# Finish of the attention heads: scaling one head further ahead, output added two heads behind, and a weight ring of eight slots

## The reference, cut to what matters

```python
def xattn(inputs_q, inputs_kv, Wq, Wk, Wv, Wo):
    q = (inputs_q @ Wq).reshape(b, sq, H, HD) * (1.0 / np.sqrt(HD))
    k = (inputs_kv @ Wk).reshape(b, skv, H, HD)
    v = (inputs_kv @ Wv).reshape(b, skv, H, HD)
    attn = softmax(einsum('bqhd,bkhd->bhqk', q, k), axis=-1)
    ctx = einsum('bhqk,bkhd->bqhd', attn, v).reshape(b, sq, H * HD)
    return ctx @ Wo

x = x + xattn(layernorm(x), ctx_2048, Wq, Wk, Wv, Wo)
x = x + linear_attn(layernorm(x), log_decay, ...)   # chunk of 128 rows, gate, group norm
x = x + ffn(layernorm(x), w1, b1, ln_g, ln_b, w2, b2)
```

## Time and profile before

| | before |
|---|---|
| median of 3 runs | 2038.02 us (2037.34 to 2038.19) |
| profiled execution | 2039.78 us |
| its span, first to last instruction | 2037.9 us |
| TensorE busy | 1955.8 us (96%) |
| VectorE busy | 1606.4 us (79%) |
| ScalarE busy | 1127.4 us (55%) |
| GpSimd busy | 272.4 us (13%) |
| mean rate of DMA over the span | 149 GB/s |

### The profile page before, as it was taken

How to read it: one execution, slowest core, us unless ns; L and a number is a source line. 1 busy time by engine, 2 the same in 40 slices (tenths; PEclk the granted TensorE clock), 3 DMA queues, 4 the chain that set the end, 5 groups by cost and what they waited for, 6 DMA issues and landing times.

```text
span 2037.9 us, 46247 instructions
## 1 busy us (share of the span) xinstructions
PE 1955.8 (96%) x17334; PEld 1596.3 (78%) x17334; DVE 1606.4 (79%) x3444; ACT 1127.4 (55%) x2484; POOL 272.4 (13%) x465
## 2 busy tenths in 40 slices
PE   5799999999999999999999999999999999999786
PEld 5577887887887987977978978878878878878462
DVE  4788788788888888888888888888888887877426
ACT  3556566666656555555555565555565556555212
POOL 1011111111111111111111111111111111100001
PEclk8899999999999999999999999999999999999888
DMA  5568887887886888787787887888978877765540
GB/s 147 148 113 163 164 162 153 160 165 153 163 161 133 143 161 162 145 160 156 146 165 156 147 156 156 147 155 162 168 147 157 147 136 142 138 121 128 206 177 6
DMA packets 966945, 304.44 MB, mean 149 GB/s; under 512 B 893985, under 2 KB 952865, under 8 KB 965825
## 3 DMA queue, kind: packets, MB, share of 16 engines
q1 hardware_dynamic: 966720, 301.47, 74.8%
HBM read 72.16 MB, written 4.46 MB: 38 GB/s over the span
## 4 chain that ended last, share of the span: by engine, by line
PE 91%; DVE 5%; DMA 2%; issue 1%; ACT 1%; POOL 0%; DVEq 0%; ACTq 0%; SPq 0%; POOLq 0%
PE ps_v L1211 25%; PE ps_s L1196 24%; PE ps_t L1196 19%; PE ps_w L1211 18%; DMA bulk<-in_vo 1%; PE ps_w L1170 1%; DVE pp L875 1%; PE ps_v L1183 1%; PE ps_t L1290 1%; DVE acc L884 0%; PE ps_s L1333 0%; PE ps_v L1297 0%; DVE prob L870 0%; ACT bulk L602 0%; PE ps_s L1152 0%
## 5 line engine op out<-in xcount | busy, mean ns | idle before, releaser
L1196 PE MATMUL ps_s<-bulk 128*128 128x128 f16 (+2 forms) x4752 | 583.4, 272 | 2.7 <-DVE bulk L811 2.7
L1211 PE MATMUL ps_v<-nring,pt 128*128 128x256 f16 x4704 | 581.4, 273 | 3.0 <-DVE acc L884 1.5
L1211 PEld LDWEIGHTS ps_v<-nring,pt 128*128 128x128 f16 x4704 | 458.8, 98 | 63.7 <-DVE acc L794 2.6
L1196 PEld LDWEIGHTS ps_s<-bulk 128*128 128x128 f16 x4752 | 404.6, 98 | 114.7 <-DVE bulk L811 2.9
L1196 PE MATMUL ps_t<-bulk 128*128 128x384 f16 (+2 forms) x3564 | 454.0, 272 | 18.9 <-ACT ps_t L653 17.2
L1211 PE MATMUL ps_w<-nring,pt 128*128 128x256 f16 x3528 | 451.8, 273 | 8.0 <-DVE ps_w L894 6.4
L875 DVE SCALAR_TENSOR_TENSOR pp<-prob,pp 128x384 f16<-128x384 f32 (+4 forms) x680 | 423.5, 689 | 0.0
L1196 PEld LDWEIGHTS ps_t<-bulk 128*128 128x128 f16 x3564 | 301.8, 98 | 111.6 <-ACT ps_t L653 18.9
L1211 PEld LDWEIGHTS ps_w<-nring,pt 128*128 128x128 f16 x3528 | 340.0, 98 | 57.5 <-DVE ps_w L894 8.6
L633 ACT ACTIVATE pp<-prob 128x384 f16<-128x384 f32 (+4 forms) x680 | 370.9, 623 | 5.5 <-DVE prob L870 4.7
L622 ACT ACTIVATE prob<-ps_s,nmax 128x768 f32<-128x768 f32 (+2 forms) x136 | 119.1, 876 | 431.6 <-DVE nmax L850 424.9
(11 more groups left out here) (187 smaller groups left out, 1410.5 us busy)
## 6 DMA issues: line engine op xcount, KB each, us to landing
stage<-in_ctx SPq DMA_DIRECT2D x196, 128.0 KB, 2.9
wst<-in_w SPq DMA_DIRECT2D x64, 256.0 KB, 3.2
bulk<-in_vo SPq DMA_DIRECT2D x16, 512.0 KB, 6.4
acc<-in_qk SPq DMA_DIRECT2D x11, 512.0 KB, 4.1
pt<-pp SPq DMA_TRANSPOSE x272, 5.6
tern_d<-wter SPq DMA_DIRECT2D x32, 128.0 KB, 2.9
bulk<-tern_d SPq DMA_DIRECT2D x2, 2048.0 KB, 11.1
nring<-in_aw SPq DMA_DIRECT2D x3, 1024.0 KB, 8.4
```

Source lines behind the costliest of these rows:

```text
L1196: ins = mm(out if n == 1 else out.rearrange("p (n m) -> p n m", m=P), q_part(e, qlo, a)[:, c * P:(c + 1) * P], t_moving(k, run, tlo, b, c) ...
L1211: ins = mm(dst, pt[:, tile:tile + P], n_part(c, clo, b), start=(first and n == 0 and plo == 0 and clo == 0), stop=(last and n == w - 1 and ...
```

## The change

It touches only the end of the attention and the loads that feed it.

- VectorE scales heads 0 and 1 before its part of the last step (135), and later head f+2 before it copies head f. `norm_head` waits for the last step of its own pair in place of the last of all.
- TensorE takes `turn(2)` and `finish(1)` ahead of the values of step 134, and `turn(3)` and `finish(2)` ahead of those of step 135. `add_out` runs two heads behind `finish`, and starts at f = 3. `ot` has three buffers, which lie in `part_u`.
- The weight ring has eight slots. The first five are loaded after step 130, three more after step 132, the others when their slot is free. The `aw` matrices but the last are mixed with the next loads; the last, the feed-forward weights and the rows come after all heads' weights. `aw_q` and one of the rows lie in `pt` now.
- The decay matrix's operations come two heads later on VectorE and ScalarE.

```diff
-        un, ut, ot = prob[:, 0:2 * D], prob[:, 2 * D:4 * D], prob[:, 4 * D:4 * D + 2 * P]
-        VO = TRW + 3 * QSW
-        AQ = VO + 4 * SL
+        un, ut, ot = prob[:, 2 * D:4 * D], prob[:, 4 * D:6 * D], part_u[:, 0:3 * P]
+        VO, NVO = TRW + 3 * QSW, 8
         tern = bulk[:, 0:WP * D].bitcast(BF16)
         b1b, lngb = (bulk[:, WP * D + n * F:WP * D + (n + 1) * F] for n in range(2))
-        ring_vo = bulk[:, VO:AQ]
-        lnbb = bulk[:, AQ:AQ + F]
-        aw_q = bulk[:, AQ + F:AQ + F + KC * D]
+        ring_vo = bulk[:, VO:VO + NVO * SL]
+        aw_q, lnbb = (pt[:, n * 2 * F:(n + 1) * 2 * F].bitcast(F32) for n in range(2))
...
+        def last_step(e):
+            return max(k for k, step in enumerate(STEPS) if step[0] == e)
...
             def load_vo(f):
-                if f >= 4:
-                    sp.wait_ge(out_mm, f - 3)
-                sp.dma_start(ring_vo[:, (f % 4) * SL:(f % 4 + 1) * SL], vo_d[Q_ORDER[f]]).then_inc(in_vo[f % 4], 16)
+                if f >= NVO:
+                    sp.wait_ge(out_mm, f - NVO + 1)
+                sp.dma_start(vo_slot(f), vo_d[Q_ORDER[f]]).then_inc(in_vo[f % NVO], 16)
...
-                if k == NS - 2:
-                    sp.wait_ge(s4_done, max(i for i, step in enumerate(STEPS) if step[0] == 5) + 1)
-                    for f in range(4):
+                if k == last_step(5) + 1:
+                    sp.wait_ge(s4_done, last_step(5) + 1)
+                    for f in range(5):
+                        load_vo(f)
+                if k == last_step(7) + 1:
+                    sp.wait_ge(s4_done, last_step(7) + 1)
+                    for f in range(5, NVO):
                         load_vo(f)
...
+            for f in range(NVO, NVO + 3):
+                load_vo(f)
+            sp.wait_ge(v4_done, NS)
             sp.dma_start(aw_q, aw_d[0]).then_inc(in_aw, 16)
-            load_vo(4)
-            sp.wait_ge(v4_done, NS)
-            for n, w in enumerate((aw_k, aw_v, aw_o)):
+            for n, w in enumerate((aw_k, aw_v)):
+                load_vo(NVO + 3 + n)
                 sp.dma_start(w, aw_d[n + 1]).then_inc(in_aw2[n], 16)
-                load_vo(5 + n)
             sp.dma_start(xin, x_d).then_inc(in_xr, 16)
-            load_vo(8)
+            for f in range(NVO + 5, H):
+                load_vo(f)
+            sp.dma_start(aw_o, aw_d[3]).then_inc(in_aw2[2], 16)
             for n in range(2):
                 sp.wait_ge(out_w[n], 16 * WP)
-            for f in range(9, H):
-                load_vo(f)
-                if f in (11, 13):
-                    n = (f - 11) // 2
-                    sp.dma_start(tern[:, n * WP * D:(n + 1) * WP * D].rearrange("p (n d) -> p n d", d=D),
-                                 tern_d[n * WP:(n + 1) * WP].rearrange("n p d -> p n d")).then_inc(in_tern, 16)
+                sp.dma_start(tern[:, n * WP * D:(n + 1) * WP * D].rearrange("p (n d) -> p n d", d=D),
+                             tern_d[n * WP:(n + 1) * WP].rearrange("n p d -> p n d")).then_inc(in_tern, 16)
...
-                if f == 0:
-                    value_a(NS - 2)
-                    value_e_u(NS - 2)
-                    value_a(NS - 1)
-                    value_e_u(NS - 1)
-                if f == 6:
+                if f in (2, 3):
+                    value_a(NS - 4 + f)
+                    value_e_u(NS - 4 + f)
+                if f == 8:
...
-            for k in range(NS):
+            for k in range(NS - 1):
                 step(k)
-            v.wait_ge(lo_done, 5 * NS)
...
-                if f == 0:
-                    v.wait_ge(l_done, 2 * alphas(NS - 1))
+                final = last_step(h // 2)
+                v.wait_ge(l_done, 2 * alphas(final))
                 for g in range(2):
-                    v.wait_ge(acc_done[g], NS - LAG if f < 2 else NS)
+                    v.wait_ge(acc_done[g], final + 1)
...
             def o_copy(f):
                 v.wait_ge(o_mm, f + 1)
-                if f >= 2:
-                    v.wait_ge(out_mm, f - 1)
-                nc.vector.tensor_copy(ot[:, (f % 2) * P:(f % 2 + 1) * P], ps_t[:, (f % 2) * D:(f % 2) * D + P]).then_inc(o_cp, 1)
-
+                if f >= 3:
+                    v.wait_ge(out_mm, f - 2)
+                nc.vector.tensor_copy(ot[:, (f % 3) * P:(f % 3 + 1) * P], ps_t[:, (f % 2) * D:(f % 2) * D + P]).then_inc(o_cp, 1)
+
+            v.wait_ge(lo_done, 5 * (NS - 1))
             norm_head(0)
             norm_head(1)
-            o_copy(0)
-            value_sum_d(NS - 2)
-            value_sum_e(NS - 2)
-            add_values(NS - 2, 1)
-            add_values(NS - 2, 0)
-            value_sum_d(NS - 1)
-            value_sum_e(NS - 1)
-            add_values(NS - 1, 1)
-            add_values(NS - 1, 0)
-            norm_head(2)
-            o_copy(1)
-
-            v.wait_ge(in_const, 16 * 5)
+            step(NS - 1)
...
-            for f in range(2, H):
-                if f + 1 < H:
-                    norm_head(f + 1)
+            for f in range(H):
+                if f + 2 < H:
+                    norm_head(f + 2)
                 o_copy(f)
-                if f < 6:
-                    nc.vector.tensor_tensor(dec3[:, f - 2], diff3, ld3[:, f - 2].to_broadcast([P, 4, P]), ALU.mult).then_inc(dec_p, 1)
-                elif 8 <= f < 12:
+                if f in (1, 2):
+                    k = NS - 3 + f
+                    value_sum_d(k)
+                    value_sum_e(k)
+                    add_values(k, 1)
+                    add_values(k, 0)
+                if 4 <= f < 8:
+                    v.wait_ge(in_const, 16 * 5)
+                    nc.vector.tensor_tensor(dec3[:, f - 4], diff3, ld3[:, f - 4].to_broadcast([P, 4, P]), ALU.mult).then_inc(dec_p, 1)
+                elif 10 <= f < 14:
                     v.wait_ge(dec_e, 1)
-                    nc.vector.tensor_tensor(dec3[:, f - 8], dec3[:, f - 8], mask3, ALU.mult).then_inc(dec_m, 1)
+                    nc.vector.tensor_tensor(dec3[:, f - 10], dec3[:, f - 10], mask3, ALU.mult).then_inc(dec_m, 1)
...
             turn(0)
             turn(1)
             finish(0)
-            values(NS - 2)
-            values(NS - 1)
             for f in range(1, H):
                 if f + 1 < H:
                     turn(f + 1)
                 finish(f)
-                if f == 1:
+                if f in (1, 2):
+                    values(NS - 3 + f)
+                if f == 3:
                     pe.wait_ge(acc_done[1], NS)
-                add_out(f - 1)
+                    pe.wait_ge(acc_done[0], NS)
+                    add_out(0)
+                if f == 4:
+                    add_out(1)
+                if f >= 4:
+                    add_out(f - 2)
+            add_out(H - 2)
             add_out(H - 1)
```

More of the change, by code:

```diff
@@ L252, in alphas, with vo_slot @@
             return sum(visit(i) > 0 for i in range(k + 1))
+        def vo_slot(f):
+            return ring_vo[:, (f % NVO) * SL:(f % NVO + 1) * SL]
+        def last_step(e):
+            return max(k for k, step in enumerate(STEPS) if step[0] == e)
         Q_ORDER = [h for k in range(NP) for h in heads_of(k)]
@@ L259, in perceiver_layer @@
         in_qk = [sem(f"in_qk{k}") for k in range(3)]
-        in_vo = [sem(f"in_vo{k}") for k in range(4)]
+        in_vo = [sem(f"in_vo{k}") for k in range(NVO)]
         in_ctx = sem("in_ctx")
@@ L1281, in finish @@
             def finish(f):
[L1282 to L1283 removed]
+                w = vo_slot(f)
+                pe.wait_ge(in_vo[f % NVO], 16 * (f // NVO + 1))
                 pe.wait_ge(exp_done[1], NS)
```

6 lines of the change are left out of this document (2 added, 4 removed).

## The result

| | before | after |
|---|---|---|
| median of 4 runs | 2037.68 us (2036.57 to 2038.19) | 2015.07 us (2013.23 to 2015.53) |
| profiled execution, its span | 2039.78, 2037.9 us | 2015.33, 2013.5 us |

The ratio is 0.9886, with a 95% interval of 0.9870 to 0.9901: 22.6 us faster, where 23.3 was forecast (2014.7). A second set of runs of the same kernel had a median of 2013.86 us.

The account below looks back on a forecast made before the run. TensorE was taken to bound, idling behind head scaling (11.2 us) and weights (5.3 us), with clock drops. Input rows added at 1935.6 instead of 1958.90 gave 2037.9 - 23.3 = 2014.6 us span, 2014.7 off the median; 8-in-10 range 2010.5 to 2021.0.

Parts of the forecast that it names:

- Scaling ahead of step 135: VectorE before step 135: scaling heads 0 and 1 puts 1.28 us on the path; step 133's values end at 1888.95.
- First heads and the values: TensorE at the heads' start: `finish(1)` ends 1893.5, second set of values starts 1898.5, `add_out(0)` starts 1903.5.
- Price of a head: TensorE's loop over heads: 2.40 us per head, between 2.31 and 3.13; rival of 3.13 us, chance 0.07.
- ScalarE at head 9: ScalarE's exponential over 2048 columns delays the copy of head 9: a fraction of a us, once.
- Weights and rows in time: Last head's load ends 1926.6 to 1930.8, `finish(15)` begins 1931.8; spread rows hidden; rival of late loads, chance 0.06.
- Transposes of step 131: Behind five earlier loads: landings 1 us later, at 1858.8 and 1860.5; no cost, 0.8 us to spare.
- The clock: TensorE's clock during the heads: 1.00 throughout; rival of drops costing over 3 us, chance 0.09.
- The tail: Linear attention and feed-forward after the input rows are added: some 79 us, as the 79.0 before.
- theory A: Longer idle products in the tail: pauses just ahead let the clock fall; filled, both products run at 1.00, tail 77.1 us.

Follow-up runs that it names:

- the order alone: New order of the heads on the three compute engines, with the ring of four and old load order of the kernel before: 2036.31 us, 0.9988 of before.
- the late scaling: Changed kernel with heads 0 and 1 scaled after step 135 again: 2016.17 us, 0.9890 of before.
- the idle products in before: Kernel before with 16 idle TensorE products ahead of `turn(0)`: 2037.15 us, 0.9991 of before.
- the feed-forward weights: Changed kernel with the two 2048 KB feed-forward loads ahead of the weights of heads 13 and 14: 2025.87 us, 0.9933 of before.
- the longer idle products: Changed kernel with two groups of idle TensorE products in the tail lengthened, 16 to 23 and 28 to 34: 2013.29 us; with the gaps 2009.95 us.
- the gaps: Changed kernel with heads 0 and 1 scaled in VectorE's idle time of steps 133 and 134: 2012.17 us, 0.9866 of before.
- the ring alone: Ring of eight and new order of loads, with the heads in the order of the kernel before: 2030.70 us, 0.9957 of before.

## Why the prediction was right

The mechanisms were those that it named. Its steps, in its order:

- *Scaling ahead of step 135*: 1.28 us on the path. The pause went from 0.27 to 1.46 us, so 1.19, and step 133's values ended at 1888.82, for 1888.95 forecast.
- *First heads and the values*: `finish(1)` at 1892.45, the first values at 1893.34 (1893.5 forecast), the second at 1898.34 (1898.5), `add_out(0)` at 1903.18 (1903.5).
- *Price of a head*: the mis-sized term. It was put at 2.40 us, bounded below by 2.31; it is 2.19, with 2.56 once. I took the duration of a row (1.02) for the step from `add_out` to what follows, and 0.49 for a `turn`, which was its step behind a wait. Unhindered they are 0.86 and 0.44: the rows overlap, as a `turn` of 0.60 us is followed by `finish` 0.44 after its start. The kernel before had shown the 0.44 once, from 1909.61 to 1910.05. The bound failed in part for the same reason, since 3.70/4 divides a group's whole duration; with the last product's 1.02 taken off it would be 0.89, still above 0.86. Ten heads give 1907.16 to 1929.43, 22.3 us for 24.0, and this is most of the 2.5 us by which the input rows were added early.
- *ScalarE at head 9*: a fraction of a us, once. 0.3 us.
- *Weights and rows in time*: yes, with less cover than the step gave. It looked at the last head alone, whose weights landed at 1927.9 (1926.6 to 1930.8 forecast), 1.6 us ahead of `finish(15)`; head 13 had 0.2 us. A head of 2.19 us uses the weights up faster than one of 2.40. The queue moved 347 to 380 GB/s, all loads were in by 1951.2, and VectorE first used a spread row at 1960.58 without a wait, 27.5 us after the input rows.
- *Transposes of step 131*: right in that they cost nothing, wrong in the working. The landings were put 1 us later, at 1858.8 and 1860.5. The first took 4.33 us to issue in place of 1.85 and landed at 1859.7; the second was issued at 1857.79, 2.4 us later than before, and landed at 1861.8. By the prediction's account, with both due before 1861.27, this would have been a wait. But ScalarE's write of each part of `pp` waits only for that part's own transpose (`in_pt[g]`): the first part was written again from 1861.23, the second from 1862.27. That left 1.5 and 0.5 us.
- *The clock*: 1.00 through all of the heads (1889 to 1937). The Trainium skill (TensorE: Matmul & The Clock Gate, A second HAM failure mode: psum-queue depth-cycling) tells of micro-idles in another kernel that keep the clock falling. Neither the loop with 0.72 us idle per head (1910 to 1946 in before) nor the new one shows it: both held 1.00. The prediction's list of before's falls lacks the third, 1950.4 to 1957.3. Its sum did not need it, since it builds the new path from its start.
- *The tail*: put at 79.0 unchanged; 80.4. It was taken as fixed, and it is not: before had one fall of 10.2 us in its first half (1981.1 to 1991.4), after three of 3.4 us (1957.2, 1967.5 and 1981.1), which met other products, L1374 and L1396.

The gain to the input rows was 2.5 us larger and the tail 1.4 us longer, and before's profiled execution lay 1.76 us over the median of 2038.02 that the forecast started from, where after's lay 0.26 over its own: these cancelled. That 2014.7 came so near to 2015.07 is luck; the terms were off by 1.4 to 2.5 us each.

Of my expectations, the one for the order alone failed. I had the added waits for weights at too little, because I had not asked what a faster TensorE demands of a queue that still carries 4.2 MB for later in the midst. Others had the mechanism and missed the size: the late scaling (2.5 us for 3 to 3.5), the idle products in before (0.9 us of the median for 2 to 2.5) and the feed-forward weights (11 to 12 us for 6 to 9). And the longer idle products, with and without the gaps, brought tails of 78.3 and 79.8 us where theory A had 77.1.

## What to carry to other kernels

Look for the copy or scaling that the producer makes only after it has waited for the consumer: moving it one iteration ahead removes the cycle. But cost it together with the transfers that the faster loop will need; here the order alone was worth 2.5 us, the ring alone 8, both 22.6. A table without waits for loads does not tell how much cover is left: compare the landing of every load with its first use, not only of the last. Take the price of a loop from the starts of successive rows, not from their durations.
